# Gated cross-attention block with experts: masked key blocks for the row maxima replaced by two-head key blocks and queries masked twice

## What is computed

```python
q = (layernorm(x) @ Wq + bq)   # 16 heads of 16 channels
k = (y @ Wk + bk); v = (y @ Wv + bv)
attn = softmax(einsum('bnhd,bmhd->bhnm', q, k) * scale)
out = einsum('bhnm,bmhd->bnhd', attn, v)
x = x + tanh(g_xattn) * (relu(out @ W1 + b1) @ W2 + b2)
# 8 experts, the two best per token, weights floored and normalised
x = x + tanh(g_ffn) * mixture_of_experts(layernorm(x))
```

## Time and profile before

| what | value |
|---|---|
| median of 3 runs | 1013.13 us (1012.97 to 1013.41) |
| the profiled execution | 1012.68 us |
| its span in the profile | 1011.0 us |
| busy share of PE, PEld | 93%, 69% |
| busy share of DVE, ACT, POOL | 82%, 71%, 64% |

### The profile page before, as it was taken

How to read it: one execution, slowest core, us unless ns; L and a number is a source line. 1 busy time by engine, 2 the same in 40 slices (tenths; PEclk the granted TensorE clock), 3 DMA queues, 4 the chain that set the end, 5 groups by cost and what they waited for, 6 DMA issues and landing times.

```text
span 1011.0 us, 26189 instructions
## 1 busy us (share of the span) xinstructions
PE 945.1 (93%) x9410; PEld 692.7 (69%) x9410; DVE 824.9 (82%) x2134; ACT 721.1 (71%) x1517; POOL 651.8 (64%) x856
## 2 busy tenths in 40 slices
PE   2758999999999999999999999999999999999997
PEld 2546677777767777776777777677777777777763
DVE  3566888888888888888888888888888888888875
ACT  4556787777778777777877777787777778777661
POOL 4435566777666677766667776666777666677643
PEclk9977999999999999999999999999999999999999
DMA  6000000000000000000000000000000000000000
GB/s 207 14 11 4 15 24 25 25 22 15 25 15 25 24 25 22 15 25 15 25 24 25 22 15 24 14 25 25 25 23 15 25 14 25 25 12 11 12 13 21
DMA packets 17472, 24.62 MB, mean 24 GB/s; under 512 B 2798, under 2 KB 8896, under 8 KB 17344
## 3 DMA queue, kind: packets, MB, share of 16 engines
q1 hardware_dynamic: 17344, 22.94, 7.1%
HBM read 14.54 MB, written 8.39 MB: 23 GB/s over the span
## 4 chain that ended last, share of the span: by engine, by line
PE 68%; POOL 11%; ACT 9%; issue 7%; DVE 3%; DMA 1%; SPq 0%; POOLq 0%; DVEq 0%; ACTq 0%
PE e L711 21%; PE g L711 20%; PE t L894 9%; POOL p_lo L372 6%; POOL k_block L426 5%; PE t L760 5%; PE s L845 4%; ACT qsT L606 3%; ACT scaled L621 2%; PE g L720 2%; ACT p_hi L545 2%; PE s L780 1%; PE g L856 1%; PE s L781 1%; PE s L782 1%
## 5 line engine op out<-in xcount | busy, mean ns | idle before, releaser
L372 POOL TENSOR_TENSOR p_lo<-p_f,p_hi 77x512 f16<-77x512 f32 x160 | 183.2, 1161 | 234.3 <-ACT p_hi L545 234.3
L711 PE MATMUL e<-we_hi,x2T_lo 128*128 128x512 f16 x496 | 188.9, 381 | 0.0
L711 PE MATMUL e<-we_hi,x2T_hi 128*128 128x512 f16 x496 | 188.4, 380 | 0.0
L711 PE MATMUL e<-we_lo,x2T_hi 128*128 128x512 f16 x496 | 188.4, 380 | 0.0
L544 ACT ACTIVATE p_f<-t 77x512 f32<-77x512 f32 x256 | 151.9, 593 | 24.8 <-PE t L760 24.4
L1156 DVE SCALAR_TENSOR_TENSOR acc<-e,comb,acc 128x256 f32<-128x256 f32 x307 | 145.9, 475 | 14.1 <-PE e L711 11.8
L545 ACT ACTIVATE p_hi<-t 77x512 f16<-77x512 f32 x256 | 151.9, 593 | 0.0
L1201 DVE TENSOR_REDUCE row_max<-s 128x6 f32<-128x462 f32 (+1 forms) x192 | 108.0, 576 | 11.4 <-PE s L845 11.4
L780 PEld LDWEIGHTS s<-v_hi,p_lo 77*128 77x128 f16 x1024 | 83.3, 96 | 32.2 <-issue 19.5
L780 PE MATMUL s<-v_hi,p_lo 77*128 77x17 f16 x1024 | 97.8, 172 | 5.2 <-POOL p_lo L372 2.5
L426 POOL TENSOR_TENSOR k_block<-own_head,khT 128x616 f16<-128x616 f16 x64 | 95.1, 1488 | 5.7 <-ACT khT L575 5.7
(11 more groups left out here) (189 smaller groups left out, 2924.0 us busy)
## 6 DMA issues: line engine op xcount, KB each, us to landing
x_sb<-in_x SPq DMA_DIRECT2D x32, 256.0 KB, 2.6
out<-acc SPq DMA_DIRECT2D x32, 256.0 KB, 2.0
we_f<-in_L_ffn_expert_W SPq DMA_DIRECT2D x2, 1024.0 KB, 9.2
y_sb<-in_ctx SPq DMA_DIRECT2D x32, 57.8 KB
w_f<-in_L_xattn_W SPq DMA_DIRECT2D x2, 512.0 KB
wq_f<-in_L_xattn_Wq SPq DMA_DIRECT2D x1, 256.0 KB
wkv_f<-in_L_xattn_Wk SPq DMA_DIRECT2D x1, 192.0 KB
wkv_f<-in_L_xattn_Wv SPq DMA_DIRECT2D x1, 192.0 KB
```

What stands on the lines that cost most here:

```text
L372: pool.tensor_tensor(p_lo[:, r].rearrange("m h n -> m (h n)"), p_f[:, r, :], p_hi[:, r].rearrange("m h n -> m (h n)"), ALU.subtract).then_ ...
L711: mm = pe.matmul(out_ap, a, c, start=(i == 0), stop=(i == n - 1))
```

## The change

Place h in the new order of the heads stands for half k = h // 8, parity e = h // 4 % 2 and block g = h % 4. Block g of `k_quad` holds the 32 partitions g * 32 to g * 32 + 31, the channels of two neighbouring heads; all else in it is zeroed once at the start. The queries are copied twice, once with the channels of the odd heads set to zero and once with those of the even ones: ScalarE multiplies by a column of `parity` (0 or 1 per partition). A product of one copy with four blocks gives four heads. So `khT`, `k_block` and GpSimd's products are gone, ScalarE makes six copies where it made two, and the first chunk of six heads is now two matmuls. Heads stand in another order in `row_max`, which the two stacking functions undo with their patterns. The core of the diff:

```diff
 EPS, W_THRES, TOP_K = 1e-4, 0.1, 2
 SCALE = float(DH) ** -0.5
 
-MAX_CHUNKS = [[(0, 6)], [(6, 2), (8, 4)], [(12, 4)]]
+MAX_CHUNKS = [[(0, 4), (4, 2)], [(6, 2), (8, 4)], [(12, 4)]]
 EARLY = 7 + 5
-CONSTS = EARLY + 1 + 7
+CONSTS = EARLY + 1 + 8
 PARTS = 4
 POOL_LOW = (1, 3, 4, 5, 6)
 VECTOR_LOW = (0, 2, 7)
...
         ffn_scale = sb("ffn_scale", [P, 1])
         ident32 = sb("ident32", [P, P])
         ident16 = sb("ident16", [P, P], F16)
-        own_head = sb("own_head", [P, PAIRS, M], F16)
+        own_head, parity = sb("own_head", [P, PAIRS]), sb("parity", [P, 2])
         beat_from = sb("beat_from", [P, T, E, E])
         zeros = sb("zeros", [P, T, E])
         minus_half, ln_eps = sb("minus_half", [P, T]), sb("ln_eps", [P, T])
...
         k_hi, q_hi = sb("k_hi", [M, D], F16), sb("q_hi", [P, T, D], F16)
         k_stack = sb("k_stack", [M, H, SLOT], F16)
         q_stack = sb("q_stack", [P, T, H, SLOT], F16)
-        qhT = sb("qhT", [P, KC, N], F16)
-        khT = sb("khT", [P, KC, M], F16)
-        k_block = sb("k_block", [P, H, M], F16)
+        qhT = sb("qhT", [P, 2, KC, N], F16)
+        k_quad = sb("k_quad", [P, KC, P // QUAD, M], F16)
         row_max = sb("row_max", [P, T, H])
         kz = sb("kz", [P, PAIRS, 2, M], F16)
         qsT = sb("qsT", [P, PAIRS, N], F16)
...
                 pool.wait_ge(v_split, 2 * b + 1)
                 pool.tensor_tensor(v_lo[:, u, :, 0:DH], v, v_hi[:, u, :, 0:DH], ALU.subtract).then_inc(v_split, 1)
 
-            def key_blocks(b, c):
-
-                pool.wait_ge(khT_done, b + 1)
-                at_least(pool, max_scores, 6 * b)
-                pool.tensor_tensor(k_block[:, c * PAIRS:(c + 1) * PAIRS, :], own_head[:],
-                                   khT[:, c, :].unsqueeze(1).to_broadcast([P, PAIRS, M]),
-                                   ALU.mult).then_inc(k_block_done, 1)
-
             pool.wait_ge(x_loaded[0], 16)
             first_norm_scale(0)
             pool.affine_select(out=beat_from[:], in_=beat_from[:], compare_op=ALU.is_gt, fill=0.0, base=0,
...
             pool.memset(k_stack[:, :, SHIFT + 2:SLOT], 0.0).then_inc(consts_ready, 1)
             pool.memset(q_stack[:, :, :, SHIFT + 2:SLOT], 0.0).then_inc(consts_ready, 1)
             pool.memset(kz[:], 0.0).then_inc(consts_ready, 1)
+            pool.memset(k_quad[:], 0.0).then_inc(consts_ready, 1)
 
             pool.memset(v_hi[:, :, :, DH:DV], 1.0).then_inc(consts_ready, 1)
             pool.memset(v_lo[:, :, :, DH:DV], 0.0).then_inc(consts_ready, 1)
...
                 if has(s, -1):
                     for g in POOL_LOW:
                         p_low(m, g)
-                if has(s, 0):
-                    key_blocks(b, 0)
                 if has(s, -2):
                     stack_comb(e, eu)
                 if has(s, 0):
-                    key_blocks(b, 1)
                     k_low(b)
                 if has(s, -3):
                     add_scaled(f, fu)
...
 
             def highT_copies(b):
                 act.wait_ge(hiT_in_psum, b + 1)
-                at_least(act, k_block_done, 2 * b)
                 at_least(act, max_scores, 6 * b)
+                if b == 0:
+                    act.wait_ge(consts_ready, CONSTS)
+                    act.wait_ge(parity_ready, 1)
                 src = G_HIGH[:].bitcast(F16)
-                act.activation(khT[:], src[:, KC * N:KC * (N + MP)].rearrange("p (k m) -> p k m", k=KC)[:, :, 0:M],
-                               ACT.Copy).then_inc(khT_done, 1)
-                act.activation(qhT[:].rearrange("p k n -> p (k n)"), src[:, 0:KC * N], ACT.Copy).then_inc(qhT_done, 1)
+                khT = src[:, KC * N:KC * (N + MP)].rearrange("p (k m) -> p k m", k=KC)
+                for g in range(P // QUAD):
+                    rows = slice(g * QUAD, (g + 1) * QUAD)
+                    act.activation(k_quad[rows, :, g, :], khT[rows, :, 0:M], ACT.Copy).then_inc(k_quad_done, 1)
+                for e, done in enumerate((even_done, qhT_done)):
+                    act.activation(qhT[:, e].rearrange("p k n -> p (k n)"), src[:, 0:KC * N], ACT.Copy,
+                                   scale=parity[:, e:e + 1]).then_inc(done, 1)
 
             def oT_high(b):
                 act.wait_ge(oT_in_psum, b + 1)
...
 
                 t, c = divmod(i, len(MAX_CHUNKS))
                 if i == 0:
+                    pe.wait_ge(k_quad_done, 4 * b + 4)
+                    pe.wait_ge(even_done, b + 1)
                     pe.wait_ge(qhT_done, b + 1)
-                    pe.wait_ge(k_block_done, 2 * b + 1)
-                if i == 1:
-                    pe.wait_ge(k_block_done, 2 * b + 2)
                 if i < 2:
                     at_least(pe, o_done, 4 * b - 2 + 2 * i)
                 else:
                     pe.wait_ge(max_taken, 6 * b + i - 1)
                 at = 0
                 for h, n in MAX_CHUNKS[c]:
-                    mm = pe.matmul(S[i % 2][:, at * M:(at + n) * M], qhT[:, h // PAIRS, t * P:(t + 1) * P],
-                                   k_block[:, h:h + n, :], start=True, stop=True)
+                    k, e, g = h // PAIRS, h // 4 % 2, h % 4
+                    mm = pe.matmul(S[i % 2][:, at * M:(at + n) * M], qhT[:, e, k, t * P:(t + 1) * P],
+                                   k_quad[:, k, g:g + n, :], start=True, stop=True)
                     at += n
                 mm.then_inc(max_scores, 1)
 
...
 
             first_norm_stats(0, 0, 0)
             first_norm_sums(0)
+            dve.wait_ge(consts_ready, EARLY)
+            dve.tensor_reduce(parity[:], own_head[:].rearrange("p (g e) -> p e g", e=2), AX.X, ALU.add).then_inc(parity_ready, 1)
 
             dve.wait_ge(first_loaded, 16 * FIRST)
             dve.wait_ge(tanh_ready, 1)
...
 
                 dve.wait_ge(max_taken, 6 * b + 6)
                 at_least(dve, qs_in_psum, 2 * b)
-                flat = q_stack[:].rearrange("p t h r -> p (t h) r")
-                mx = row_max[:].rearrange("p t h -> p (t h)")
-                dve.tensor_copy(flat[:, :, SHIFT], mx).then_inc(max_hi_done, 1)
+                flat = q_stack[:].rearrange("p t (k g e) r -> p (t k) e g r", g=4, e=2)
+                mx = row_max[:].rearrange("p t (k e g) -> p (t k) e g", g=4, e=2)
+                dve.tensor_copy(flat[:, :, :, :, SHIFT], mx).then_inc(max_hi_done, 1)
 
             def stack_max_low(b):
-                flat = q_stack[:].rearrange("p t h r -> p (t h) r")
-                mx = row_max[:].rearrange("p t h -> p (t h)")
+                flat = q_stack[:].rearrange("p t (k g e) r -> p (t k) e g r", g=4, e=2)
+                mx = row_max[:].rearrange("p t (k e g) -> p (t k) e g", g=4, e=2)
                 dve.wait_ge(max_hi_done, b + 1)
-                dve.tensor_tensor(flat[:, :, SHIFT + 1], mx, flat[:, :, SHIFT], ALU.subtract).then_inc(max_lo_done, 1)
+                dve.tensor_tensor(flat[:, :, :, :, SHIFT + 1], mx, flat[:, :, :, :, SHIFT], ALU.subtract).then_inc(max_lo_done, 1)
 
             def oT_low(b):
                 dve.wait_ge(oT_hi_done, b + 1)
```

More of the change, by code:

```diff
@@ L193, in gated_block @@
         q_hi_done, q_lo_done, q_stacked = sem("q_hi_done"), sem("q_lo_done"), sem("q_stacked")
-        hiT_in_psum, qhT_done, khT_done = sem("hiT_in_psum"), sem("qhT_done"), sem("khT_done")
-        k_block_done = sem("k_block_done")
+        hiT_in_psum, qhT_done, even_done, k_quad_done = sem("hiT_in_psum"), sem("qhT_done"), sem("even_done"), sem("k_quad_done")
+        parity_ready = sem("parity_ready")
         max_scores, max_taken = sem("max_scores"), sem("max_taken")
@@ L332, in _ @@
             pool.affine_select(out=own_head[:], in_=own_head[:], compare_op=ALU.is_ge, fill=0.0, base=0,
-                               pattern=[[-DH, PAIRS], [0, M]], channel_multiplier=1).then_inc(consts_ready, 1)
+                               pattern=[[-DH, PAIRS]], channel_multiplier=1).then_inc(consts_ready, 1)
             pool.wait_ge(consts_ready, 6)
             pool.affine_select(out=own_head[:], in_=own_head[:], compare_op=ALU.is_ge, fill=0.0, base=DH - 1,
-                               pattern=[[DH, PAIRS], [0, M]], channel_multiplier=-1).then_inc(consts_ready, 1)
+                               pattern=[[DH, PAIRS]], channel_multiplier=-1).then_inc(consts_ready, 1)
             pool.memset(minus_half[:], -0.5).then_inc(consts_ready, 1)
```

## The result

The changed kernel takes 1052.87 us (median of 4 runs, 1051.83 to 1053.59) against 1013.05 us of the kernel before in the same job: 1.0393 times as long, 95% interval 1.0375 to 1.0411. The forecast was 1029.9 us, range 1019.5 to 1035.5: the sign was right, but the loss of 39.8 us was more than twice the one forecast, and the time lies outside the range.

The account below looks back on a forecast made before the run. TensorE, 93% busy, was taken as the bound. Steady steps 15.1 us, step 1 1.8, step 2 0.4, step 0 -0.5 gave +16.8 on the profiled 1012.68; with the median 0.45 higher, 1029.9 us, range 1019.5 to 1035.5.

Parts of the forecast that it names:

- Six copies on ScalarE, four of them held: ScalarE before the first product for the maxima: partition changes cost the overlap; each steady step gets 0.52 us longer, 15.1 us.
- t0: Start of ScalarE's key copy in a step; the first product for the maxima was to move from 2.17 to 2.69 behind it.
- 0.14 us from ScalarE's end to TensorE: Time from the end of ScalarE's last query copy to TensorE's first product for the maxima, read from another product.
- ScalarE's stacks covered in a steady step, 1.8 us in step 1, 0.4 in step 2, -0.5 in step 0: ScalarE's query and key stacks come 1.78 us later; idle 2.06 us covers that in steps 3 to 31, start-up steps differ.
- 64 more matmuls cost nothing: TensorE's products for the maxima: 154 and 308 columns in a pair take 0.20 us, as one matmul of 462 does.
- Everything behind them in GpSimd's queue moves up, but nobody on TensorE waits for those pieces in a steady step.: GpSimd without its two key blocks a row: only the removed wait is gained; the earlier queue counts for nothing.
- The rivals: Three other outcomes: no change (1011.9 us, chance 0.12), faster (1006.5, 0.05), heavier (1034.0, 0.05).
- C, the heavier one: ScalarE's odd query copy starts only after the even one ends: 0.14 us a step more, 4.1 us, 1034.0; chance 0.05.
- the closing caution: The prediction would be wrong if something behind the maxima gave the delay back, the period growing by less than the wait.
- the first place: TensorE's wait before the first product for the maxima, forecast to grow from 0.53 to 1.05 us a step.

Follow-up runs that it names:

- a_rows: The changed kernel with all four key copies from and to partitions 0 to 31, leaving the maxima wrong: 1034.21 us, one run.
- a_noscale: The changed kernel with the two query copies made without the parity scale, so no head is masked: 1047.84 us, one run.
- a_sem: The changed kernel with all six ScalarE copies counted on one semaphore: 1046.81 us, 1.0319 times the kernel before.
- a_xb: The changed kernel with GpSimd's xb addition moved ahead of the scale of the first norm: 1031.89 us, 1.0174 times the kernel before.

## Why the prediction was wrong

- *Six copies on ScalarE, four of them held.* Right: 2.51 us from t0 against 2.55; shown by a_rows (the hold, 0.13 to 0.14 a copy) and a_noscale (the scale, 0.09 a copy). A copy of 32 partitions took 0.28 to 0.29 us, as assumed.
- *0.14 us from ScalarE's end to TensorE.* Too small by 0.12. It was taken from a product with other waits; a_sem showed that it depends on the waits of the product (0.26 with four semaphores, 0.05 with two). This is 0.1 us a step, the smaller part of the miss.
- *ScalarE's stacks covered in a steady step, 1.8 us in step 1, 0.4 in step 2, -0.5 in step 0.* The cover held: ScalarE still idles 0.92 us ahead of the output copy. As changes of the distance to the next step 1.9, 0.8 and -0.7 were measured, but this contains xb and h_lo too. With xb early it is 1.3, 0.3 and -0.7, with one semaphore besides 1.8, about 0 and -0.9. Together that is 2.0 in the changed kernel and 0.9 with xb early, where 1.7 was forecast; that the first three numbers come near the forecast is in part luck, and no run separates the terms.
- *64 more matmuls cost nothing.* Right: 308 and 154 columns take 0.20 us (525.53 to 525.73), as 462 did.
- *"Everything behind them in GpSimd's queue moves up, but nobody on TensorE waits for those pieces in a steady step."* This is the step that failed: the move of GpSimd's queue was put at nothing. Nobody waits for xb; but an h_lo of VectorE that starts beside it does not end before it, and TensorE waits for h_lo. It cost 0.70 us a step (a_xb), 21 us, and is all of the miss of 23 us but 2. The trace before showed the neighbours: 0.21 us lie between the last h_lo and xb. The forecast moved TensorE 0.5 us back, and with it h_lo, and GpSimd forward (xb by 1.1 us, from 12.40 to 11.25 behind the first key copy), without asking what would then lie on what. The Trainium skill says ("GPSIMD Engine Reference", section "1. Specifications") that GpSimd shares its SBUF interfaces with VectorE, with contention for VectorE instructions that have two SBUF inputs. The trace agrees: h_lo has two such inputs, and it took 1.44 us instead of 0.42.
- *The rivals.* None of the three named this. C, the heavier one, looked for a longer hold on ScalarE, and the closing caution for something that gives the delay back, not for something that adds to it. That the direction was right is owed to the first place, not to luck: with xb out of the way (a_xb) the kernel takes 1031.89, 1.7% more than the kernel before, where 1029.9 was forecast.

## What to carry to other kernels

When work leaves an engine or a wait gets longer, everything behind it slides against the other engines. For each piece of GpSimd that moves, look what VectorE does with two SBUF inputs at its new time, and the other way round: in this kernel a piece that nobody waits for cost 0.7 us a step, more than the whole wait for the key blocks (0.53 us) that the change removed. And a wait in front of a product can be hidden by putting independent work ahead of it; follow it through to the next wait. Here that took a second reordering, on VectorE, since after the first the wait appeared again one product on.

## What the runs showed of the hardware that was not expected

- A VectorE subtraction of 128 x 256 with two SBUF inputs that starts beside a GpSimd addition of 128 x 512 ends 0.28 to 0.29 us behind it, in three kernels (1.44, 1.34 and 1.72 us instead of 0.41 to 0.48). Behind GpSimd's shorter `v_hi` and `v_lo` it ends as late (0.61 and 0.48 us in the kernel before).
- ScalarE loses the overlap of about 0.11 us with the instruction before, and 0.02 more, when its input and output start in another group of 32 partitions (a_rows).
- TensorE starts 0.05 us behind ScalarE's last copy when it waits for two semaphores and 0.26 behind it when it waits for four. Which of the semaphores, and in which order, makes the difference was not tried.
